# A stack of passes in which the attention operands get a new row order and new loads, and the maxima of two heads go to the two 64-row halves of the array

## The reference

```python
scores = jnp.einsum('bqhd,bkhd->bhqk', Q, K) / math.sqrt(D_K)   # first attention
scores = jnp.where(causal, scores, -jnp.inf)
attn = jax.nn.softmax(scores, axis=-1)
out = jnp.einsum('bhqk,bkhd->bqhd', attn, V)
...
num = jnp.einsum('bhtf,bhtfd->bhtd', phi_q, kv_cum)             # second attention, causal sums
den = jnp.einsum('bhtf,bhtf->bht', phi_q, jnp.cumsum(phi_k, axis=2))[..., None] + EPS
```

## Time and profile before

| | |
|---|---|
| median of 3 runs | 3066.28 us (3065.55 to 3077.27) |
| the profiled execution: its time, its span | 3066.84 us, 3065.1 us |
| busy, share of the span | PE 83%, DVE 74%, ACT 58%, POOL 18% |
| softmax attention pass | about 262 to 1314 us |
| second attention pass | about 2173 to 2797 us |

### The profile page before, as it was taken

The page is one execution under the profiler, slowest core; times in us unless marked ns, Lnnn a source line. Parts: engine busy times, 40 slices in busy tenths (PEclk is TensorE's granted clock), DMA queues, the critical chain, the costliest instruction groups (busy, mean ns, idle before and its releaser), DMA issues. The chain is left out here.

```text
span 3065.1 us, 60134 instructions
## 1 busy us (share of the span) xinstructions
PE 2551.7 (83%) x15239; PEld 1169.3 (38%) x15239; DVE 2267.6 (74%) x5886; ACT 1785.7 (58%) x2938; POOL 542.2 (18%) x636
## 2 busy tenths in 40 slices
PE   2784989889898998955999997887499999996656
PEld 1441333333333333334566665554122222222545
DVE  5896777778777777646677776999466666665978
ACT  0450566556665666621777774766377777773446
POOL 0341111111111111122000000222222222222300
PEclk9896899989999999978999998999699999998879
DMA  5587464544545445233000000444888888882403
GB/s 163 169 270 165 76 95 70 92 81 81 93 70 93 80 81 92 46 132 108 1 0 0 0 0 28 151 151 158 162 140 139 140 139 137 142 140 83 150 20 109
DMA packets 289396, 309.97 MB, mean 101 GB/s; under 512 B 40496, under 2 KB 243968, under 8 KB 276992
## 3 DMA queue, kind: packets, MB, share of 16 engines
q1 hardware_dynamic: 289280, 308.81, 48.0%
HBM read 181.29 MB, written 126.88 MB: 101 GB/s over the span
## 5 line engine op out<-in xcount | busy, mean ns | idle before, releaser
L818 ACT ACTIVATE a_p<-psum 128x1024 f32<-128x1024 f32 (+3 forms) x768 | 590.0, 814 | 384.2 <-PE psum L921 383.8
L871 DVE CUSTOM_DVE_ANT_0 a_dump<-psum,a_bias 128x256 bf16<-128x256 f32 (+3 forms) x1024 | 451.7, 487 | 175.1 <-PE psum L911 149.0
L911 PE MATMUL psum<-a_ks,a_qs 96*128 96x512 bf16 (+3 forms) x1536 | 469.0, 351 | 131.1 <-DMA a_vs<-values 107.3
L818 ACT ACTIVATE b_p<-psum 128x512 f32<-128x512 f32 (+5 forms) x768 | 453.5, 654 | 167.4 <-PE psum L921 166.5
L921 PE MATMUL psum<-a_qs,a_ks 98*128 98x512 bf16 (+3 forms) x1536 | 395.6, 341 | 5.4 <-ACT a_p L818 3.7
L869 DVE TENSOR_REDUCE a_peak<-psum 128x1 f32<-128x512 f32 x512 | 333.7, 686 | 39.1 <-PE psum L911 37.7
L921 PE MATMUL psum<-b_qs,b_ks 96*128 96x512 bf16 (+3 forms) x1536 | 320.5, 331 | 39.1 <-DMA b_vs<-values 38.8
L935 PE MATMUL psum<-a_p,a_vs 128*32 128x512 f32 (+3 forms) x3072 | 349.3, 529 | 0.6 <-POOL a_p L797 0.4
L845 DVE COPY b_twin<-psum 128x512 f32<-128x512 f32 (+3 forms) x384 | 213.5, 556 | 173.8 <-PE psum L921 172.2
L935 PE MATMUL psum<-b_p,b_vs 128*32 128x512 f32 (+3 forms) x3072 | 328.5, 500 | 8.0 <-POOL b_p L797 8.0
L911 PEld LDWEIGHTS psum<-a_ks,a_qs 96*128 96x128 bf16 x1536 | 135.8, 100 | 495.7 <-issue 155.4
(11 more groups left out here) (187 smaller groups left out, 3263.4 us busy)
## 6 DMA issues: line engine op xcount, KB each, us to landing
qk_parts<-l_parts SPq DMA_DIRECT2D x192, 128.0 KB
a_qs<-qk_parts SPq DMA_DIRECT2D x192, 128.0 KB, 4.7
a_ks<-qk_parts SPq DMA_DIRECT2D x192, 128.0 KB, 7.4
qk_parts<-g_parts SPq DMA_DIRECT2D x192, 128.0 KB, 1.7
b_qs<-qk_parts SPq DMA_DIRECT2D x192, 128.0 KB, 4.7
b_ks<-qk_parts SPq DMA_DIRECT2D x192, 128.0 KB, 8.0
values<-l_vx SPq DMA_DIRECT2D x64, 256.0 KB
a_vs<-values SPq DMA_DIRECT2D x32, 512.0 KB, 9.7
```

Of the source, the lines that this page charges most:

```text
L818: act.activation(p[s % SLOTS][:, 2 * k:2 * k + heads, q0(s):512], m.psum[:, at:at + heads, q0(s):512], ACT.Exp if softmax else ACT.Square, ...
L871: last = dve.tensor_tensor_reduce(dump[c % SRING][:, at:at + w], piece, bias[:, 512 - w:], 1.0, NEG, ALU.add, ALU.max, dst)
L911: last = pe.matmul(m.bank[SB + c % SRING][:, at:at + w], qs[r][0:STACK, hd, qt * P:(qt + 1) * P], ks[r][0:STACK, hd, h * 512:h * 512 + w], ...
```

## The change

Each part of Q and K gets another slot in DRAM (`Q_SLOT`, `K_SLOT`), so that neighbouring slots can be loaded in one DMA to 32 partitions, part and row interleaved. The six products still stand in 96 rows, but in an order in which the four that serve the maxima of heads 0 and 1 lie in rows 0 to 63, and three that serve those of heads 2 and 3 in rows 64 to 111. Rows that then hold nothing are set once, to zero or one, by DVE at the start of both attention passes; loads and TensorE wait for it. The rows of the maxima move to 112 and 113. The values lie in DRAM by partition. The maxima are computed by pairs of heads (0 with 2, 1 with 3), one pair of chunks in every second slot, each chunk in its own half of the array; 9 pairs of each unit come early (`EARLY`), and the wait for the load stands in slot 19.

```diff
-Q_STACK = ((0, 0, 3), (1, 0, 2), (2, 0, 1))
-K_STACK = ((0, 1, 3), (0, 1, 2), (0, 1, 1))
+Q_SLOT = (1, 2, 0)
+K_SLOT = (1, 0, 2)
 STACK = 16 * 6
+MAIN = 16 * 4
+TOP = 16 * 7
...
-        self.v_dram = nc.dram_tensor("values", [z.UNITS, z.S, P], F32, kind="Internal").ap()
+        self.v_dram = nc.dram_tensor("values", [z.UNITS, P, z.ST, P], F32, kind="Internal").ap()
...
+        def operand_rows(hd):
+
+            if softmax:
+                return slice(0, TOP + 2)
+            return slice(0, STACK) if hd < HPU // 2 else slice(0, TOP)
...
             def load(n, r):
-                for tile, which, stack in ((qs[r], 0, Q_STACK), (ks[r], 1, K_STACK)):
-                    row = 0
-                    for first, step, groups in stack:
-                        for part in range(groups):
-                            src = m.qk_dram[first + step * part, which, bass.ts(n, HPU * z.DK), :]
-                            sp.dma_start(tile[row:row + z.DK, :, :].rearrange("p h t -> p (h t)"),
-                                         src.rearrange("(d h) t -> d (h t)", h=HPU)).then_inc(loaded[r], 16)
-                            row += z.DK
+                if not isinstance(n, int) or n >= RING:
+                    sp.wait_ge(rows_set, RING)
+                else:
+                    sp.wait_ge(rows_set, n + 1)
+                q, k = [tile[:, :, :].rearrange("p h t -> p (h t)") for tile in (qs[r], ks[r])]
+                parts = [m.qk_dram[:, which, bass.ts(n, HPU * z.DK), :].rearrange("g (d h) t -> d g (h t)", h=HPU)
+                         for which in range(2)]
+                half = z.S * HPU // 2
+                for par, runs in enumerate((((0, 1, 2, 0, 2), (32, 2, 2, 0, 2), (64, 0, 0, 1, 2)),
+                                            ((64, 1, 2, 0, 2), (96, 2, 1, 1, 1), (0, 2, 1, 0, 1), (16, 0, 0, 1, 2)))):
+                    heads = slice(par * half, (par + 1) * half)
+                    for row, q_slot, q_wide, k_slot, groups in runs:
+                        into = slice(row, row + z.DK * groups)
+                        src = parts[0][:, q_slot:q_slot + (1 if q_wide else groups), heads]
+                        if q_wide:
+                            src = src.to_broadcast([z.DK, groups, half])
+                        sp.dma_start(q[into, heads], src).then_inc(loaded[r], 16)
+                        sp.dma_start(k[into, heads], parts[1][:, k_slot:k_slot + groups, heads]
+                                     ).then_inc(loaded[r], 16)
...
         def _(dve):
+            for r in range(RING):
+                for tile, fill in ((qs[r], 0.0), (ks[r], 1.0)):
+                    dve.memset(tile[32:MAIN, HPU // 2:HPU, :], 0.0)
+                    last = dve.memset(tile[STACK:P, 0:(HPU if softmax else HPU // 2), :], fill)
+                last.then_inc(rows_set, 1)
...
-            for r in range(RING):
-                last = dve.memset(ks[r][STACK:STACK + 2, :, :], 1.0)
-            last.then_inc(ones_ready, 1)
...
-            if softmax:
-                pe.wait_ge(ones_ready, 1)
+            pe.wait_ge(rows_set, RING)

             def maximum_scores(n, r, a, b):
...
+                for j in range(a, b):
+                    for par in range(2):
+                        pe.wait_ge(s_taken, CH * n + 2 * j + par + 1)
+                        for piece, (qt, h, at, w) in enumerate(chunks[j][1]):
+                            hd, half = chunks[j][0] + par * HPU // 2, (slice(0, MAIN), slice(MAIN, TOP))[par]
+                            last = pe.matmul(m.bank[SB + (2 * j + par) % SRING][:, at:at + w],
+                                             qs[r][half, hd, qt * P:(qt + 1) * P],
+                                             ks[r][half, hd, h * 512:h * 512 + w], start=True, stop=True)
+                            if piece == len(chunks[j][1]) - 1:
+                                last.then_inc(s_ready, 1)
...
-                    half = CH // 2
-                    if k < half and ahead:
-                        maximum_scores(n + 1, (r + 1) % RING, half + k, half + k + 1)
...
+                    j = k // 2
+                    if j < CP - EARLY and ahead:
+                        maximum_scores(n + 1, (r + 1) % RING, EARLY + j, EARLY + j + 1)
```

More of the change, by code:

```diff
@@ L651, in store_parts @@
         for j in range(4):
-            eng.dma_start(m.qk_dram[part, j // 2, bass.ds(i * z.D + (j % 2) * P, P), u * z.GT:(u + 1) * z.GT],
+            slot = (Q_SLOT, K_SLOT)[j // 2][part]
+            eng.dma_start(m.qk_dram[slot, j // 2, bass.ds(i * z.D + (j % 2) * P, P), u * z.GT:(u + 1) * z.GT],
                           parts[:, part, j, :]).then_inc(stored, 16)
@@ L675, in attend_pass @@
     SLOTS = 4
-    chunks = [(hd, pieces) for hd in range(HPU) for pieces in (
+    chunks = [(hd, pieces) for hd in range(HPU // 2) for pieces in (
         ((0, 0, 0, 128), (2, 0, 128, 384)), ((3, 0, 0, 512),), ((1, 0, 0, 256), (5, 1, 256, 256)),
@@ L682, in attend_pass @@
         ((7, 0, 0, 512),), ((7, 1, 0, 512),))]
-    CH = len(chunks)
+    CP = len(chunks)
+    CH = 2 * CP
     assert CH == 3 * STEPS
     SRING = 3
+    EARLY = 9
     with ExitStack() as ctx:
@@ L862, in maxima @@
             def maxima(n, a, b):
-                for c in range(a, b):
-                    hd, pieces = chunks[c]
+                for c in range(2 * a, 2 * b):
+                    hd, pieces = chunks[c // 2][0] + c % 2 * HPU // 2, chunks[c // 2][1]
                     wait_alone(dve, s_ready, CH * n + c + 1, m.alone)
@@ L889, in unit @@
                 if ahead:
[L890 removed]
+                    maxima(n + 1, EARLY, CP)
                     largest(n + 1, (rows_loaded[r], ROWS_LOADED * rnd + ROWS_LOADED))
                 if far:
[L893 to L895 removed]
+                    maxima(n + 2, 0, EARLY)
+            maxima(0, 0, CP)
             largest(0, None)
[L897 removed]
+            maxima(1, 0, EARLY)
             all_units(dve, unit)
@@ L920, in scores @@
                 for hd in (2 * k, 2 * k + 1):
-                    last = pe.matmul(m.bank[score_bank(s, hd)][:, q0(s):512], ks[r][0:ROWS, hd, kt * P:(kt + 1) * P],
-                                     qs[r][0:ROWS, hd, h * 512 + q0(s):(h + 1) * 512], start=True, stop=True)
+                    live = operand_rows(hd)
+                    last = pe.matmul(m.bank[score_bank(s, hd)][:, q0(s):512], ks[r][live, hd, kt * P:(kt + 1) * P],
+                                     qs[r][live, hd, h * 512 + q0(s):(h + 1) * 512], start=True, stop=True)
                 last.then_inc(st_ready, 1)
@@ L946, in some_maxima @@
                 def some_maxima(k):
-                    if not softmax:
+                    if not softmax or k % 2 == 0:
                         return
-                    half = CH // 2
-                    if k < half and ahead:
-                        maximum_scores(n + 1, (r + 1) % RING, half + k, half + k + 1)
-                    if k >= half and far:
-                        if k == half:
+                    j = k // 2
+                    if j < CP - EARLY and ahead:
+                        maximum_scores(n + 1, (r + 1) % RING, EARLY + j, EARLY + j + 1)
+                    if j >= CP - EARLY and far:
+                        if j == CP - EARLY:
                             pe.wait_ge(loaded[(r + 2) % RING], LOADED * (rnd + (r + 2) // RING) + LOADED)
-                        maximum_scores(n + 2, (r + 2) % RING, k - half, k - half + 1)
+                        maximum_scores(n + 2, (r + 2) % RING, j - CP + EARLY, j - CP + EARLY + 1)
                 for s in range(STEPS):
```

21 lines of the change are left out of this document (10 added, 11 removed).

## The result

The changed kernel takes 2989.34 us (median of 4 runs, 2981.57 to 2996.51) against 3068.57 us for the kernel before in the same session: a ratio of 0.9746 (0.9725 to 0.9767). The forecast was 2989, in a range of 2920 to 3070. The profiled execution has a span of 2987.6 us, 77.5 shorter than before.

A forecast was written before the change was run, and what follows sets the result against it. TensorE was taken to set the softmax loop's pace, with DVE some 7 us a unit behind. A unit loses 2.9 us, -88 over 30 units, and memsets add 10: -78, so 2989 us, range 2920 to 3070.

The forecast's parts named there:

- The load's end: Softmax loop: the load lands 11.8 us after its first issue, where it took 15.7, so 2.42 us a unit of waiting goes.
- in time by 1.3 us: Softmax loop: the load lands at 11.8 us, before TensorE comes to its wait at 13.1 us after the first issue.
- The clock: Softmax loop: clock loss falls from 1.9 to 0.6 us a unit, left only after DVE's stall; 1.3 goes.
- The pairs: Softmax loop, per unit: overlap saves 3.5 us, 24 more array changes cost 2.9, second weight loads cost 0.9.
- Own work: TensorE's own work in a softmax-loop unit: from 26.5 to 26.8 us, bounds 23.0 and 29.4.
- The coupling: Softmax loop: pairs waiting on DVE for banks, and on the maxima's rows, add 0.5 us a unit.
- the forecast's four parts: Softmax unit before: own work 26.5, load wait 2.42, DVE wait 0.73, clock 1.9; sum 31.55 of 31.80 us.
- The memsets: Starts of both attention passes: DVE's longer memsets add 9 us in the first and 1 in the second, bounds 8 and 20 together.
- Pairs for nearly nothing: Rival, softmax loop: weight loads hidden, a change 0.06 us, DVE holds the unit near 26.8; 2927 us, chance 0.16.
- The halves don't run together: Rival, softmax loop: no overlap of the pair's halves, own work 29.4 us, unit 31.5; 3067 us, chance 0.10.
- the load gets no faster: Rival, softmax loop: the load stays at 131 GB/s, wait 1.7 us, unit 31.4; 3065 us, chance 0.10.
- a change costs 0.24: Rival, softmax loop: array changes cost double and halves don't overlap, unit 34.4 us; 3155 us, slower, chance 0.12.

The follow-up runs named there:

- e1: Kernel before with the new slots, Q and K in six DMAs to 32 partitions plus the values, old order, no added memsets: 2928.45 us, ratio 0.9565.
- e3: Changed kernel with both matmuls of a pair over all 112 rows, so no halves: 2985.29 us, ratio 0.9752.
- e7: Changed kernel with both halves of a pair waiting for both banks before the first starts: 2998.86 us, ratio 0.9793.
- e5: The loads alone (seven issues, 96 full rows, no added memsets) with the changed kernel's order by pairs: 2964.39 us, ratio 0.9684.
- e8: Changed kernel with the memsets of the Q tiles on GpSimd and those of the K tiles on DVE: 2982.3 us, ratio 0.9731.
- e4: The loads alone (seven issues, old order) with the maxima over rows 0 to 63, unpaired: 3242.59, 3227.33, 3109.91 and 3382.86 us, no ratio.

## Why the prediction was right

The total came out, and so did the place: everything is gained at the load's wait and its clock in the softmax loop, and the pairs bring nothing (e1, e3). That it came out to the microsecond is luck, since two errors of over 1 us a unit met. By its steps:

- **The load's end.** Forecast 11.8 us with issues hidden at 0.48 each; measured 13.7, with 15 issues at 0.68 each on average and the values landing 4.1 us behind the last. The rate of 32 partitions came out (215 forecast, a mean of 212 in e1); the issues were the term that was mis-sized. TensorE came to its wait 12.9 us after the first issue (721.79 - 0.86 - 708.05), near the 13.1 forecast. So the load's wait fell to 0.72 us a unit, not to 0, and "in time by 1.3 us" was the step that failed. e1 shows what was left there: its seven issues take the wait away.
- **The clock.** Forecast loss 0.6 us a unit; measured 0.98, so 0.57.
- **The pairs.** Overlap, forecast 3.5 us a unit: the row of 0.32 for a pair shows it whole. Changes, forecast 24 x 0.12 = 2.9; at 0.105 they are 2.5. The second weight load, forecast half open for 0.9: it is hidden. The sign given for this, second matmuls less than 0.15 us behind the first, holds where DVE is in time, in about three pairs of four. Own work so would be 26.5 - 3.5 + 2.5 = 25.5 where 26.8 was forecast, worked out, not measured; e7, where no half is late, leaves 25.6 (28.88 less 1.88 and 0.52 of waits and 0.91 of clock, by the 51 us that the trace grants 0.50).
- **The coupling.** Forecast 0.5. The unit of 28.71, less waits of 0.72 and 0.88 and 0.57 of clock, leaves 26.5, not 25.5. The missing 1.0 and the 0.15 by which the wait on DVE grew, are the coupling: in full it is 1.2, more than twice the forecast. The missing 1.0 is late second halves as the one at 726.27: the trace has 1.6 us a unit of them beside the brackets, and e7, which has none, leaves 25.6. The sum is not exact to better than half a microsecond. With full rows the order by pairs loses time in the same way (0.52 in e5).
- **The two errors** met: 0.72 of a wait that stayed and 0.65 more coupling than forecast, against 1.3 less of own work. What is left of the difference lies in the 0.25 that the forecast's four parts left open in the unit before. Unit: forecast 28.9, measured 28.71.
- **The memsets.** Forecast +9 in the softmax pass; about 11 measured. The four fills of a slot take 7.05 us by their rows (one of zeros half of what one of ones takes, 1.76 against 3.47 us for 4096 elements), but gaps of 0.25 to 0.89 us between them make it 8.9, where 8.1 was forecast. +1 in the second pass; measured 1 to 2. Splitting them (e8) moves TensorE's start back by 9.0 us, so this is their own time.
- **The sum.** 30 x (28.71 - 31.80) = -93, starts +13: -80, and the spans differ by 77.5.
- **The rivals.** "Pairs for nearly nothing" had the weight loads right and the change (0.06) wrong, and let DVE hold the unit near 26.8, where late halves, waits and clock make it 28.71. "The halves don't run together" is out by the pair's 0.32, "the load gets no faster" by e1's 212 GB/s, and "a change costs 0.24" by e4's 0.10.

What the prediction didn't see is how much was left: the same slots with seven issues and the old order give 133 us, and the regrouping by pairs, with the fifteen issues that it needs, gives 55 to 61 of these back.

Left open: why the clock is at 0.98 in some of these kernels and at 1.00 in others (each fall in these loops stands behind a wait of TensorE, but e1 and e5 have nine long waits each, and the clock falls behind one of them in e1 and behind seven in e5); and whether the halves would pay with more banks for the maxima. No kernel with four banks was tried, and none with halves and seven issues.

## What to carry to other kernels

When a load is late, count both its ends: data by partitions reached, and issues at what they take in the very loop where they stand (0.7 us here, not the 0.48 of simpler ones). Two chunks side by side in the array save columns, but here the saving went again, where their buffers came free one by one and where other uses stood between pairs, since each change costs 0.1 us. A wait in brackets is not all that a late operand costs: what the row before it covers is missing there. And try each part of a change both alone and undone: here two causes held the loop at the same length, and undoing either showed nothing.

## What the runs showed of the hardware

- The half clock that stays: in e4 the granted clock fell behind a wait of 1.67 us, as it falls in the other kernels, but then units ran at 0.50 with TensorE busy in 54.00 of 54 us, in an execution that had run at 1.00 with the same work shortly before. In the softmax loop of the kernel before it was 1.00 again within 11 us each time. e4 differs from e1 only in its 64 rows and their 48 changes a unit; which of them keeps the clock low was not tried.
- A change between full rows and half rows, or from half rows to the column strips, cost 0.10 to 0.11 us each; out of the column strips it was more, as a weighing of 0.85 us of columns still occupies 1.00 (718.58 to 719.58).
- DMAs to 32 partitions moved 212 GB/s on average where those to 16 moved 131, and those to 128 moved 301 to 330 in single microseconds.
